# A graph, attention and expert layer: duplicate edges removed over spans of six groups, with six table additions in flight

## The reference, cut to what matters

```python
e = jax.nn.leaky_relu(s_src[src] + s_dst[dst], NEG_SLOPE)
emax = jax.ops.segment_max(e, dst, num_segments=n)
ee = jnp.exp(e - emax[dst])
denom = jax.ops.segment_sum(ee, dst, num_segments=n)
alpha = ee / denom[dst]
out = jax.ops.segment_sum(alpha[:, :, None] * h[src], dst, num_segments=n)
...
x = x + gnn(xn) + mix(xn[None])[0]
x = x + ffn(_layernorm(x)[None])[0]
```

## Time and profile before

| what | value |
|---|---|
| median of three runs | 1384.6 us (1381.84, 1384.6, 1390.06) |
| span of the profiled execution | 1381.2 us |
| TensorE busy | 1167.6 us, 85% |
| VectorE, ScalarE, GpSimd busy | 56%, 33%, 22% |
| mean granted TensorE clock | 0.930 |

### The profile page before, as it was taken

The page is one execution under the profiler, slowest core; times in us unless marked ns, Lnnn a source line. Parts: engine busy times, 40 slices in busy tenths (PEclk is TensorE's granted clock), DMA queues, the critical chain, the costliest instruction groups (busy, mean ns, idle before and its releaser), DMA issues.

```text
span 1381.2 us, 17242 instructions
## 1 busy us (share of the span) xinstructions
PE 1167.6 (85%) x6752; PEld 1080.2 (78%) x6752; DVE 775.8 (56%) x1660; ACT 449.3 (33%) x706; POOL 307.9 (22%) x238
## 2 busy tenths in 40 slices
PE   2999999999998203995999989378879999999998
PEld 2889987799898203885988879377756999999998
DVE  7685225254464102677899954979774344544354
ACT  2533002430133201343766635177143212222111
POOL 2027776866677641001000000000000000000000
PEclk8999999999998656998999989688989999999999
DMA  7993225256413296224100000200101100111102
GB/s 254 387 356 39 35 36 137 1 142 161 106 1 58 29 296 155 70 69 145 52 0 1 1 1 29 87 0 1 47 1 46 47 14 34 47 46 46 47 1 112
DMA packets 72327, 108.23 MB, mean 78 GB/s; under 512 B 30325, under 2 KB 52197, under 8 KB 72247
## 3 DMA queue, kind: packets, MB, share of 16 engines
q1 hardware_dynamic: 41399, 74.10, 15.8%
q0 software_dynamic: 30848, 33.04, 12.2%
HBM read 82.04 MB, written 25.07 MB: 78 GB/s over the span
## 4 chain that ended last, share of the span: by engine, by line
PE 41%; DVE 19%; DMA 15%; POOL 11%; issue 11%; ACT 2%; POOLq 0%; DVEq 0%; SPq 0%; ACTq 0%
PE bank L1292 32%; POOL table L546 10%; DMA table<-match,slot_ix 8%; PE bank L1481 7%; DVE junk_m L1053 4%; DMA cnt<-table 3%; DMA keyrow<-key_d 3%; DVE pbuf L1143 3%; DVE pbuf L1117 3%; PE bank L1303 2%; DVE keyrow L933 1%; ACT vbuf L767 1%; DVE h L1126 1%; DVE sb_stats L885 1%; DVE x L1192 1%
## 5 line engine op out<-in xcount | busy, mean ns | idle before, releaser
L546 POOL DMA_INDIRECT table<-match,slot_ix x168 | 274.4, 1633 | 168.6 <-DMA table<-match,slot_ix 57.1
L1481 PE MATMUL bank<-h,pbuf 128*128 128x193 f32 (+1 forms) x1200 | 192.9, 323 | 30.3 <-DVE pbuf L1143 29.1
L1481 PEld LDWEIGHTS bank<-h,pbuf 128*128 128x128 f32 x1200 | 184.3, 200 | 38.8 <-DVE pbuf L1143 34.6
L1292 PE MATMUL bank<-f_hi,hT 128*128 128x384 f32 x640 | 166.5, 335 | 0.0
L1292 PE MATMUL bank<-w_hi,tT 128*128 128x384 f32 x480 | 131.6, 348 | 8.8 <-DVE w_lo L606 4.6
L1292 PEld LDWEIGHTS bank<-f_hi,hT 128*128 128x128 f32 x640 | 116.0, 188 | 0.5
L1053 DVE CUSTOM_DVE_ANT_0 junk_m<-a_row,pen 128x1280 bf16<-128x1280 f32 x40 | 59.7, 1492 | 94.9 <-DMA a_row<-s_d 78.0
L1274 DVE SCALAR_TENSOR_TENSOR x<-bank,sb_gate,x 128x384 f32<-128x384 f32 x160 | 93.5, 614 | 29.0 <-PE bank L1292 28.6
L1292 PE MATMUL bank<-f_lo,hT 128*128 128x384 f32 x320 | 107.0, 334 | 0.0
L1223 DVE TENSOR_TENSOR hT<-silu,hT 128x512 fp32r<-128x512 f32 (+1 forms) x48 | 28.8, 603 | 139.0 <-ACT hT L834 139.0
L1292 PE MATMUL bank<-y2T_hi,f_hi 128*128 128x512 f32 (+1 forms) x288 | 102.7, 357 | 2.8 <-DVE y2T_lo L869 2.8
(11 more groups left out here) (230 smaller groups left out, 2334.5 us busy)
## 6 DMA issues: line engine op xcount, KB each, us to landing
table<-zero POOLq DMA_DIRECT2D x2, 6400.5 KB, 42.3
cnt<-table POOLq DMA_DIRECT2D x20, 640.0 KB, 15.9
keyrow<-key_d SPq DMA_DIRECT2D x24, 448.0 KB, 8.9
w_raw<-in_kqvT SPq DMA_DIRECT2D x6, 1152.0 KB, 5.9
f_raw<-in_w1T SPq DMA_DIRECT2D x8, 768.0 KB, 4.7
f_raw<-in_w2T SPq DMA_DIRECT2D x8, 768.0 KB, 6.3
acc_d<-ubuf SPq DMA_DIRECT2D x20, 192.0 KB, 1.9
accbuf<-acc_d SPq DMA_DIRECT2D x10, 384.0 KB, 3.1
```

The lines of the kernel that those rows point to most:

```text
L546: pool.indirect_dma_start(table[g % 2], bass.IndirectOffsetOnAxis(ap=slot_ix[:, g:g + 1], axis=0), match[:, g:g + 1], None, compute_op=ALU ...
L1292: return nc.tensor.matmul(o, l, r, start=first, stop=last)
L1481: ins = nc.tensor.matmul(b[:, d * stride:d * stride + chans + 1], score[:, dt * P:(dt + 1) * P], h_t[:, st, h, 0:chans + 1], start=st == 0 ...
```

## The change

- Chunks have six groups instead of seven (28 chunks). Each group is compared with all 768 keys of its chunk instead of its own 128, so the duplicates are marked over the whole chunk. `before` becomes a band of 11 x 128 columns of which each group takes a 768-column window; the products go to two small junk tiles (uint8) instead of back in place, and a comparison waits until the one two before it is done.
- Duplicates go to a trash row of their own for each group of the chunk; the two small steps per chunk become tensor-tensor forms.
- All six additions of a chunk go into one table, with no wait between them; chunk c goes into table c % 2 and waits for chunk c - 2.
- Each table has its own semaphore for the zeroing, the first two chunks wait for their own; the wait for `consts_in` before the zeroing is gone. The zeroing source is 610 columns instead of 753.
- SP loads the fourth weight half behind key chunk 12 instead of 10.

```diff
-    KC = 7
+    KC = 6
...
-        ZW = 753
+        ZW = 610
...
+        BW = (2 * KC - 1) * P
+        before = at("before", TAIL + 8192, [P, BW])
+        junk_k = [at(f"junk_k{i}", TAIL + 8192 + 4 * BW + KC * P * i, [P, KC * P], mybir.dt.uint8) for i in range(2)]
...
-        table = [dram(f"table{i}", (TAB + P, 1)) for i in range(2)]
+        table = [dram(f"table{i}", (TAB + NT * P, 1)) for i in range(2)]
...
-                if c == 10:
+                if c == 12:
                     load_half(3)
...
+            nc.gpsimd.memset(before[:, 0:(KC - 1) * P], 1.0 + DUP).then_inc(blank_done, 1)
+            nc.gpsimd.memset(before[:, (KC - 1) * P:BW], 1.0).then_inc(blank_done, 1)
...
             pool.wait_ge(zero_done, 1)
-            pool.wait_ge(consts_in, 16 * N_CONST)
-            for tab in table:
+            for i, tab in enumerate(table):
                 view = tab.rearrange("(p a n) o -> p a (n o)", p=P, n=ZW)
-                pool.dma_start(view, zero[:, :].unsqueeze(1).broadcast_to([P, view.shape[1], ZW])).then_inc(table_zeroed, 16)
-            pool.wait_ge(table_zeroed, 32)
+                pool.dma_start(view, zero[:, :].unsqueeze(1).broadcast_to([P, view.shape[1], ZW])).then_inc(table_zeroed[i], 16)
             for c in range(NCH):
                 pool.wait_ge(slots_done, c + 1)
+                if c < 2:
+                    pool.wait_ge(table_zeroed[c], 16)
+                else:
+                    pool.wait_ge(scattered[c % 2], 16 * KC * (c // 2))
                 for g in range(c * KC, (c + 1) * KC):
-                    if g >= 2:
-                        pool.wait_ge(scattered[g % 2], 16 * (g // 2))
-                    pool.indirect_dma_start(table[g % 2], bass.IndirectOffsetOnAxis(ap=slot_ix[:, g:g + 1], axis=0),
+                    pool.indirect_dma_start(table[c % 2], bass.IndirectOffsetOnAxis(ap=slot_ix[:, g:g + 1], axis=0),
                                             match[:, g:g + 1], None, compute_op=ALU.add,
-                                            bounds_check=TAB + P - 1).then_inc(scattered[g % 2], 16)
+                                            bounds_check=TAB + KC * P - 1).then_inc(scattered[c % 2], 16)
...
                 for k in range(KC):
-                    g = c * KC + k
-                    chunk = keyrow[c % KR][:, k * P:(k + 1) * P]
+                    g, first = c * KC + k, (KC - 1 - k) * P
+                    if g >= 2:
+                        dve.wait_ge(match_done, g - 1)
                     nc.vector.scalar_tensor_tensor(
-                        out=chunk, in0=chunk, scalar=key[:, g:g + 1], in1=before[:, :],
+                        out=junk_k[g % 2][:, :], in0=keyrow[c % KR][:, :], scalar=key[:, g:g + 1], in1=before[:, first:first + KC * P],
                         op0=ALU.is_equal, op1=ALU.mult, accum_out=match[:, g:g + 1]).then_inc(match_done, 1)
...
-                nc.vector.tensor_scalar(slot_ix[:, s], key_off[:, s], trash_c[:, 0:1], None, ALU.add).then_inc(slots_done, 1)
+                nc.vector.tensor_tensor(slot_ix[:, s], key_off[:, s], trash_c[:, :], ALU.add).then_inc(slots_done, 1)
```

More of the change, by code:

```diff
@@ L60, in gps_layer @@
         ident, ones = sb("ident", [P, P]), sb("ones", [P, P])
-        before = sb("before", [P, P])
-        trash_c, trash_i = sb("trash_c", [P, 1]), sb("trash_i", [P, 1], I32)
+        trash_c, trash_i = sb("trash_c", [P, KC]), sb("trash_i", [P, KC], I32)
         junk_d = sb("junk_d", [P, C1], BF16)
@@ L201, in gps_layer @@
         match_done, slots_done = sem("match_done"), sem("slots_done")
-        zero_done, table_zeroed = sem("zero_done"), sem("table_zeroed")
+        zero_done = sem("zero_done")
+        table_zeroed = [sem(f"table_zeroed{i}") for i in range(2)]
         scattered = [sem(f"scattered{i}") for i in range(2)]
@@ L406, in _ @@
                 sp.dma_start(r[:, :], v.broadcast_to([P, D])).then_inc(consts_in, 16)
-            sp.wait_ge(blank_done, 9)
+            sp.wait_ge(blank_done, 10)
             for h in range(MH):
@@ L506, in _ @@
             nc.gpsimd.memset(zero[:, :], 0.0).then_inc(zero_done, 1)
-            for m, v in ((ident, 0.0), (before, 1.0), (ones, 1.0), (KVb, 0.0), (KVd, 0.0), (wk, 0.0), (wq, 0.0),
-                         (negk, 0.0), (negq, 0.0)):
+            for m, v in ((ident, 0.0), (ones, 1.0), (KVb, 0.0), (KVd, 0.0), (wk, 0.0), (wq, 0.0), (negk, 0.0), (negq, 0.0)):
                 nc.gpsimd.memset(m[:], v).then_inc(blank_done, 1)
-            pool.wait_ge(blank_done, 9)
+            nc.gpsimd.memset(before[:, 0:(KC - 1) * P], 1.0 + DUP).then_inc(blank_done, 1)
+            nc.gpsimd.memset(before[:, (KC - 1) * P:BW], 1.0).then_inc(blank_done, 1)
+            pool.wait_ge(blank_done, 10)
             nc.gpsimd.affine_select(out=ident[:, :], in_=ident[:, :], compare_op=ALU.not_equal, fill=1.0, base=0,
                                     pattern=[[-1, P]], channel_multiplier=1).then_inc(consts_done, 1)
-            nc.gpsimd.affine_select(out=before[:, :], in_=before[:, :], compare_op=ALU.is_ge, fill=1.0 + DUP, base=0,
+            own = before[:, (KC - 1) * P:KC * P]
+            nc.gpsimd.affine_select(out=own, in_=own, compare_op=ALU.is_ge, fill=1.0 + DUP, base=0,
                                     pattern=[[1, P]], channel_multiplier=-1).then_inc(consts_done, 1)
-            nc.gpsimd.iota(trash_i[:, :], pattern=[[0, 1]], base=TAB, channel_multiplier=1).then_inc(consts_done, 1)
+            nc.gpsimd.iota(trash_i[:, :], pattern=[[P, KC]], base=TAB, channel_multiplier=1).then_inc(consts_done, 1)
             nc.gpsimd.iota(iota8i[:, :], pattern=[[1, E]], base=0, channel_multiplier=0).then_inc(consts_done, 1)
@@ L902, in _ @@
             step(nc.vector.tensor_copy(trash_c[:, :], trash_i[:, :]))
-            step(nc.vector.tensor_scalar(key_off[:, :], key[:, :], trash_c[:, 0:1], None, ALU.subtract))
+            step(nc.vector.tensor_tensor(key_off[:, :].rearrange("p (c k) -> p c k", k=KC),
+                                         key[:, :].rearrange("p (c k) -> p c k", k=KC),
+                                         trash_c[:, :].unsqueeze(1).broadcast_to([P, NCH, KC]), ALU.subtract))
             step(nc.vector.tensor_copy(iota8[:, :], iota8i[:, :]))
```

## The result

The changed kernel takes 1428.0 us (median of four runs, 1427.08 to 1429.01) against 1385.4 for the kernel before beside it: ratio 1.0301, 95% interval 1.0272 to 1.0331. It is slower, as forecast, but by 43 us where the sum had 17, and outside the range of 1382 to 1418. Its profiled span is 1427.2 us, 46.0 above the one of before and 29.2 above the sum's 1398.0.

The account below looks back on a forecast made before the run. Product-bound on TensorE, with a stretch waiting for counts. That hole closes, a stall in V opens, counts come 11.8 + 5 = 16.8 us later: span 1381.2 + 16.8 = 1398.0, median 1401 us, range 1382 to 1418.

Parts of the forecast that it names:

- the hole of 68.6 us: TensorE's wait for the count tiles before 532.28 us; finishing the additions sooner can give at most this.
- a stall of 77.5: TensorE waits from about 153.7 to 231.2 us for V's banks, as V's evacuations queue behind the comparisons on VectorE.
- The pitch of 0.94 us: Time between starts of 768-column comparisons on VectorE, from a line through earlier rows; bounds 0.87 and 1.05 us.
- the early zeroing at nothing: Zeroing beside x, first weights and constants delays the first product by 0 to 8 us; not in the sum.
- The rows' collision: Loads of count tiles 0 to 5 meet SP's six constant rows after U: +5 us, bounds 0 and +9.
- The counts' stage: After the last x transpose: remaining loads and ten accumulations 40.3 us, plus 5.3 us for projT's and accumulator tiles' traffic.
- the clock behind the stall: TensorE returns from V's stall at half clock: some 3 us at half the speed add 1.5 us.
- Absorbed collisions: Rival, chance 0.18: loads and rows fit into gaps, or the comparison is nearer 0.87 us; 1390 us, within 0.5%.
- the fast mode: Rival, chance 0.05: the comparison runs two columns a cycle, about 0.54 us; -56 us, 1328.
- half rate: Rival, chance 0.03: a 768-column comparison takes 1.74 us, 134 us more in all; 1535.
- late additions: Rival, chance 0.02: GpSimd's additions become the bound, ending after 498 us; at 2.8 us each, 1431.
- The wait or the loads cost more: Rival, chance 0.16: comparison pitch 1.04 us adds 17 us (1418), or early zeroing delays the first product (1409).

Follow-up runs that it names:

- late zeroing: The changed kernel with the zeroing of the count tables put back behind the wait for all constants: 1412.5 us, ratio 1.0146.
- narrow comparisons: Changed kernel, late zeroing, each comparison on its own 128 columns, all edges to trash addresses: 1364.0 us with neighbouring words, 1324.4 us with spread ones.
- interleaved: Changed kernel, late zeroing, the new order, later wide comparisons moved between V's evacuations and to VectorE's later idle times: 1331.7 us; with the changed kernel's order 1344.4 us.
- the run with two in flight: Changed kernel with late zeroing and wide comparisons, but additions alternating tables, each waiting for the one two before: 1414.5 us, ratio 1.0166.
- the new order: Changed kernel with late zeroing, count tiles 0 to 5 loaded and accumulated before the wait for the last gT: 1389.0 us, ratio 0.9974.

## Why the prediction was right, and where it was wrong

**The direction, and the main term.** That the hole of 68.6 us closes and a stall of 77.5 opens in V was right: 76.07 us with late zeroing, and TensorE back at 231.07 against 231.2. The pitch of 0.94 us from the line through the earlier trace rows was exact, and the wait for the comparison two before cost nothing. The runs with narrow comparisons (no stall, 1324) and with interleaved ones (17 us of stall, 1344 with the count tiles in the changed kernel's order, 1332 in the new) show that this stall is what turns a gain into a loss: the gain without it is 47 us in the interleaved kernel with the old order, and 68 with narrow comparisons.

**The step that failed: the early zeroing at nothing.** The prediction put it among the rivals as "0 to 8" us because "x tiles are due late enough", and left it out of the sum and out of the range. It measured 18.0 us at the first comparison, 23.3 at the first K product (38.80 before) and 16.2 at the end; with it taken back, the kernel takes 1412.5 us, which the range has. The mechanism was named, its size wrong, for two reasons that the runs show. The x tiles were the wrong thing to look at: TensorE was done with their transposes at 39.2 us (38.8 before). SP's queue decides. Its 25 small issues took 32 us instead of 16, but this alone costs little: with half of the zeroing early they end almost as late, and the first comparison is 1.9 us behind the one with late zeroing. What costs is that the zeros still run when rw_raw (21.1 us to landing) and the two weight halves (15.11 us of issue) come. And the effect isn't on one transfer alone: rw_raw, the last of the constants, holds TensorE's first K product and VectorE until 62 us, and the first comparison then waits another 7.11 us for the key rows, whose loads stand behind the weight halves on SP.

**The rows' collision.** Forecast +5 with bounds 0 and 9; measured 10.4 us at TensorE by the run with two in flight, just outside the bounds, and VectorE's wait for the rows doubled, 7.95 to 16.27. The Trainium skill's rule that was weighed here ("DMA: Bandwidth & Descriptors", Queues, rings and completion order), turns packet by packet and so the wait doubled, agrees with this; its +8 was the better value.

**The counts' stage.** Forecast 45.6 us from the last gT, with projT's traffic in it; measured 47.6 (527.18 to 574.8). Right within 2 us, but this traffic also costs projT: TensorE waits 12.54 us for its second half (4.55 before), which the prediction didn't price. It cost little further here: TensorE takes the count tiles at 579.25 us, 4.5 after they are ready, but the first maximum waits for the score rows, which GpSimd sends after the counts.

**The sum against the trace.** From the forecast first maximum (560.7) to the measured (587.27) are 26.6 us: +18.0 start of the comparisons, -1.5 comparisons, +7.3 between TensorE's return and the last gT (279.6 us against 272.2 with the collision's 5), +2.0 counts, +0.8 score rows. Of the 7.3, 5.4 are the collision beyond its 5. Some 0.7 are the clock behind the stall, priced at 1.5 us for 3 us at half speed: the granted clock is 0.50, the lower of TensorE's two levels, after 67.57 us without a product, and stays so until 252.4 us (then the distance of starts falls from 0.32 to 0.17 us), which makes an estimated 2.2. The rest was not followed up. The window behind the stall (columns as in the earlier trace rows):

```profile
247.00:252.00 5.00, 4.37 (x14) 4.40 (x15) 5.00 (x7) 0.00 (x0) 4.39 (x3) 0.50 0.15 0
```

The 481 us at which the prediction ends the additions is the issue of the first count load; the last addition ended at 474.6. As neither was on the path after the change, this cost it nothing. Behind the first maximum another 2.6 us were lost (839.9 against 837.3); what they are wasn't followed up.

**The rivals.** Absorbed collisions, the fast mode, half rate and late additions didn't happen. "The wait or the loads cost more" did, in its second half, at twice its price.

## What to carry to other kernels

Before a long transfer is moved forward past a wait, look at the issues and loads that the wait protected: what counts is not the bytes but which transfers, on which other queue, still meet it and then hold a whole engine. Price a longer stage on one engine by the banks of the next: work that fits an engine's idle time in sum still stalls another if it stands in one piece ahead of the evacuations; moving part of it between and behind them was worth 57 us here. And a part of a change that costs nothing alone may cost most of its price once another part has used up the wait that hid it.

## What the runs showed of the hardware

- Two transfers of 6.4 MB of zeros beside them took SP's issue of an 8 KB load from 0.60 us to as much as 3.76, its landing from about 6 to 23, and the issue of two 1152 KB loads from 1.31 to 15.11 us. The issuing queue itself is held up, not only the data.
- Indirect additions to 768 neighbouring words, against ones spread 255 words apart, doubled the engines' time of another queue's unchanged traffic (31.3% to 67.4%).
- An accumulating transfer of 640 KB from HBM to SBUF took 3.07 us, a plain one 1.77; with projT's and the accumulator tiles' traffic beside them nine accumulations took 3.72 us each (540.89 to 574.34 us by the additions of loops that follow them). Taking six of them out of the stage behind the last gT was worth 11 to 13 us in the interleaved kernel. With late zeroing alone the new order gave 23, but there it also ends the collision with the constant rows.
- A comparison of 768 f32 columns with both inputs in SBUF, a uint8 output and an accumulator had a pitch of 0.94 us, the same as a form without accumulator.
